# Splitting the attention exp by head, interleaving the causal mask, and moving four projection chunks in a fused attention and FFN kernel

## The chip, the cores and the metric

The kernel runs on the 8 cores of one Trainium2 chip. Each core takes one of the 8 batch elements, with the same program and the same weights, and no data passes between the cores. The metric is the device time in microseconds (us) of the slowest core.

## The reference

One layer on x of shape (8, 2048, 1024), with 16 heads of size 64 and an FFN of width 4096:

```python
def _L0_attn_ref(x, W_qkv, W_out):
    qkv = jnp.einsum('bsd,ndh->bnsh', x, W_qkv)
    q, k, v = jnp.split(qkv, 3, axis=-1)
    attn = jnp.einsum('bnqh,bnkh->bnqk', q, k) * scale      # scale = 1/8
    mask = -1e10 * (1.0 - jnp.tril(jnp.ones((S, S))))
    attn = jax.nn.softmax(attn + mask, axis=-1)
    out = jnp.einsum('bnqk,bnkh->bnqh', attn, v)
    out = out.reshape(B, -1, S)
    return jnp.einsum('bds,nhd->bsd', out, W_out)
...
x = x + _L0_attn_ref(_layernorm(x), L0_attn_W_qkv, L0_attn_W_out)
x = x + _L0_ffn_ref(_layernorm(x), w1, b1, w2, b2)          # relu FFN
```

The last einsum of the attention sums W_out over two of its indices, so it is a multiplication of each column of the output by one number (the kernel's WB_sb).

## The kernel before

The program has three stages. Up to about 165 us it normalizes x, transposes it to lnf_sb and computes V for all heads. From there to about 750 us it does attention, which is where the change lies. Then come the second layer norm and the FFN, in four groups of 512 tokens (L716 and L762 are its two matmuls).

Attention runs over 8 pairs of heads (npair 0 to 7). A pair has 40 steps, `steps = [(qb, j) ...]`: four query blocks qb of 512 queries, and for each the key blocks j of 128 keys up to the diagonal. Block 0 has steps 0 to 3, block 1 steps 4 to 11, block 2 steps 12 to 23, block 3 steps 24 to 39. The last four steps of a block are on the diagonal: they are 512, 384, 256 and 128 queries wide, and get a mask. For each step:

- `emit_se` gives TensorE the two score matmuls (L463), one a head. Head 0 lies in partitions 0 to 63 of kpair and qpair and head 1 in partitions 64 to 127, so each matmul uses half of the rows of the array. They write two neighbouring banks of PSUM. On a diagonal step two matmuls of 128 columns (L478, maskd times the identity, 128 rows) add the mask. Then one ScalarE activation (L491) takes exp of both heads and writes p_sb, a ring of three.
- `emit_pv` gives TensorE the two matmuls of P with V (L518), 128 rows each, one a head, into banks 4 and 5. vaug_h has 64 columns of ones beside V, so that these matmuls give the sum of the softmax too.

Scores have three regions of two banks (`REG_BASE`); a region is free when the exp of its step is done. All queues are in order. The order is written out by the loop at L591: a score step is emitted while fewer than three steps are ahead of PV, otherwise the next PV. So the queue of TensorE is SE0 SE1 SE2 PV0 SE3 PV1 and so on, and PV(k) comes right before SE(k+3). (SEk and PVk are names of this text for `emit_se(k)` and `emit_pv(k)`.)

`emit_epilogue`, called after the last PV of a block, copies banks 4 and 5 to oscr_sb with two VectorE copies (L534), then ScalarE does Ln (L544) and Exp (L550) to get the reciprocal of the sums, and VectorE multiplies (L558). The first PV of the next block waits for both copies. In the queue of ScalarE the Ln and Exp of a block that ends at step n stand before the exp of step n+3.

While pair p is in work, the Q and K projections of pair p+1 are done in eight chunks of eight matmuls (L375), two chunks at a time, in region 2. They stand at four places of the order, `ck_slots`; the two matmul groups of such a place are called CK0 to CK3 here. Each is followed by four VectorE casts (L391, L398), which must be done before region 2 is used again. Before the change CK0 to CK3 stand after PV8, PV16, PV24 and PV32.

At the start of a pair VectorE copies V (L418) and applies the previous pair's result to x ("permutes", L627 and L638, four times). The copies L534 of block 0 are behind these in VectorE's queue, and PV4 waits for them. Pair 7 has no next pair and so no chunks; pair 0 has no permutes before it.

Of the kernel before, what the change touches and what calls it, by code (L numbers as in the profile page):

```python
# [9 lines left out]
AF = mybir.ActivationFunctionType  # L10
ALU = mybir.AluOpType
AP = bass.AP
# [15 lines left out]
def build_program():  # L28
# [27 lines left out]
    def add(eng, emit, waits=(), inc=None, amt=1):  # L56
        w = [wt for wt in waits if wt[1] > 0]
        seq.append((eng, w, emit, inc, amt))
        if inc is not None:
            C[inc] += amt  # L60
            return C[inc]
        return None

    with ExitStack() as ctx:
# [4 lines left out]
        identb = sb("identb_sb", [128, 128], BF16)  # L69
        maskd = sb("maskd_sb", [128, 128], BF16)  # L70
# [8 lines left out]
        cst_sb = sb("cst_sb", [128, 3], F32)  # L79
# [4 lines left out]
        qpair = asb("qpair", [128, 2, S], BF16)  # L84
        kpair = asb("kpair", [128, 2, S], BF16)
        p_sb = asb("p_sb", [128, 3, 1024], BF16)
# [5 lines left out]
        arena = ctx.enter_context(nc.psum_tensor([128, 8, 512], F32))  # L92
        AR = 8 * 512
# [5 lines left out]
        for xq in range(4):  # L99
# [4 lines left out]
                waits=([(f"dq{xq - 1}", 16)] if xq > 0 else []),  # L104
                inc=f"dq{xq}", amt=16)
            dx_xq.append((f"dq{xq}", cnt))
        add("gpsimd", lambda e: e.dma_start(identb[:, :], identf_d.ap()),
            inc="dwb", amt=16)
        add("gpsimd", lambda e: e.dma_start(b2r_sb[:, :], b2_d.ap()),
            inc="dwb", amt=16)  # L110
        dx_consts = add("gpsimd", lambda e: e.dma_start(maskd[:, :],
                                                        maskd_d.ap()),
                        inc="dx", amt=16)
        for bcc in range(NWW):
# [3 lines left out]
                inc="dbc", amt=16)  # L118
# [52 lines left out]
        for kc2 in range(DC // 2):  # L171
# [5 lines left out]
            for r in range(2):  # L177
                kc = kc2 * 2 + r
                for h in range(2):
# [5 lines left out]
                                    start=(kc_ == 0), stop=(kc_ == DC - 1),  # L185
                                    skip_group_check=True))(sp + r, h, kc),
                                waits=[dw, ("vv", vv_ones)],
                                inc="mm" if h == 1 else None)
# [4 lines left out]
            waits=[("mm", wb_mm)], inc="vv")  # L193
# [144 lines left out]
        s_reg_free = [vv_lnf1, vv_vaug_done, ("ex", 0)]  # L338
        REG_BASE = [1024, 3072, 0]
        o_bank_free = [vv_vaug_done, vv_vaug_done]  # L340
        vv_attn_done = 0
        ex_attn_done = 0
# [66 lines left out]
        for npair in range(NH // 2):  # L409
            heads = (2 * npair, 2 * npair + 1)  # L410
            par = npair % 2
# [3 lines left out]
            vv_vh = 0  # L415
            for hix, n in enumerate(heads):
                vdrain()
                vv_vh = add("vector", (lambda n_, hx: lambda e: e.tensor_copy(  # L418
                    AP(vaug_h, hx * TC * 128, [[2 * TC * 128, 128],
                                               [128, TC], [1, 64]]),  # L420
                    AP(v_all, 64 * n_, [[TC * 1024, 128],
                                        [1024, TC], [1, 64]])))(n, hix),
                    waits=[vv_vaug_done, ("vv", vv_vones),
                           vaug_free[hix]],
                    inc="vv")
            if npair + 1 < NH // 2:
                next_chunks = make_qk_chunks(
                    npair + 1,
                    load_pair_slots((2 * npair + 2, 2 * npair + 3)))
            else:  # L430
                next_chunks = []
# [6 lines left out]
            ex_exp = {}  # L438
# [3 lines left out]
            def emit_se(si):  # L442
                nonlocal ex_attn_done
                qb, j = steps[si]
                qlo = max(128 * j, 512 * qb)
                qhi = 512 * (qb + 1)
                w = qhi - qlo
                off = qlo - 512 * qb
                reg = reg_of[si]
                base = REG_BASE[reg]  # L450
                reg_prev = s_reg_free[reg]
                ppar_guard = ([("mm", mm_pv[si - 3])] if si >= 3 else
                              ([("mm", p_guard[si % 3])]
                               if p_guard[si % 3] else []))
                mm_sc = None
                for hix in range(2):
                    w0 = [reg_prev] if hix == 0 else []
                    if si == 0 and hix == 0:
                        w0.append(("vv", vv_qk_done))
                    mm_sc = add("tensor",  # L460
                                (lambda j_, q_, w_, b_, hx, off_, p_:
                                 lambda e:
                                 e.matmul(  # L463
                                     AP(arena, b_ + hx * 512 + off_,
                                        [[AR, 128], [1, w_]]),
                                     kpair[hx * 64:(hx + 1) * 64, p_,
                                           j_ * 128:(j_ + 1) * 128],
                                     qpair[hx * 64:(hx + 1) * 64, p_,
                                           q_:q_ + w_],
                                     start=True, stop=True,  # L470
                                     skip_group_check=True))(
                                     j, qlo, w, base, hix, off, par),
                                waits=w0, inc="mm" if hix == 1 else None)
                if qlo == 128 * j:
                    for hix in range(2):
                        mm_sc = add("tensor",
                                    (lambda b_, hx, off_: lambda e:
                                     e.matmul(  # L478
                                         AP(arena, b_ + hx * 512 + off_,
                                            [[AR, 128], [1, 128]]),  # L480
                                         maskd[:, :], identb[:, :],
                                         start=False, stop=True,
                                         skip_group_check=True))(
                                         base, hix, off),
                                    waits=([("dx", dx_consts)]
                                           if hix == 0 else []),
                                    inc="mm" if hix == 1 else None)
                ew = [("mm", mm_sc)] + ppar_guard
                last_ex = add("scalar",
                              (lambda si_, w_, b_, off_: lambda e:  # L490
                               e.activation(  # L491
                                   AP(p_sb, (si_ % 3) * 1024,
                                      [[3 * 1024, 128], [512, 2], [1, w_]]),
                                   AP(arena, b_ + off_,
                                      [[AR, 128], [512, 2], [1, w_]]),
                                   AF.Exp, scale=cst_sb[:, 1:2]))(
                                   si, w, base, off),
                              waits=ew, inc="ex")
                s_reg_free[reg] = ("ex", last_ex)
                ex_exp[si] = last_ex  # L500
                ex_attn_done = last_ex

            def emit_pv(si):
                qb, j = steps[si]
                qlo = max(128 * j, 512 * qb)
                w = 512 * (qb + 1) - qlo
                off = qlo - 512 * qb
                jstop = 4 * qb + 3
                last = None
                for hix in range(2):  # L510
                    w0 = [("ex", ex_exp[si])] if hix == 0 else []
                    if j == 0 and hix == 0:
                        w0.append(o_bank_free[0])
                        w0.append(o_bank_free[1])
                        w0.append(("vv", vv_vh))
                    last = add("tensor",
                               (lambda j_, w_, hx, st_, si_, off_: lambda e:
                                e.matmul(  # L518
                                    AP(arena, (4 + hx) * 512 + off_,
                                       [[AR, 128], [1, w_]]),  # L520
                                    vaug_h[:, hx, j_ * 128:(j_ + 1) * 128],
                                    AP(p_sb, (si_ % 3) * 1024 + hx * 512,
                                       [[3 * 1024, 128], [1, w_]]),
                                    start=(j_ == 0), stop=st_,
                                    skip_group_check=True))(
                                    j, w, hix, j == jstop, si, off),
                               waits=w0, inc="mm" if hix == 1 else None)
                mm_pv[si] = last
                return last
# [40 lines left out]

            s_reg_free[2] = ("vv", vv_qk_pair[npair])
            rot = []
            ck_slots = {11, 20, 29, 38} if next_chunks else set()
            si_ctr = 0
            kk = 0
            rc = 0
# [14 lines left out]
            while npv < len(steps):  # L591
# [10 lines left out]
                else:  # L602
                    emit_pv(npv)
                    qb, j = steps[npv]
# [280 lines left out]
```

How the kernel before makes its waits and increments, by code:

```python
                def body(eng_obj):  # L834
                    last_wait = {}
                    for (e, waits, emit, inc, amt) in seq:
                        if e != eng_name:
                            continue
                        for wt in waits:
                            s_, v = wt[0], wt[1]
                            force = len(wt) > 2 and wt[2]
                            if v > 0 and (force or last_wait.get(s_, -1) < v):
                                eng_obj.wait_ge(sems[s_], v)
                                last_wait[s_] = max(last_wait.get(s_, -1), v)
                        if emit is None:
                            continue
                        inst = emit(eng_obj)
                        if inc is not None:
                            inst.then_inc(sems[inc], amt)
```

## Time and profile before

| | |
|---|---|
| median of 13 runs | 1323.79 us (1320.99 to 1426.11) |
| the profiled execution | 1321.26 us; its slowest core's span is 1319.7 us |
| spans of the 8 cores | 1308.7 to 1319.7 us |
| granted TensorE clock, mean of a core | 0.858 to 0.876 |
| TensorE matmul busy | 990.5 us, 75% |
| VectorE busy | 473.2 us, 36% |
| ScalarE busy | 414.9 us, 31% |
| exp of the scores (L491) | 320 activations, 294.3 us |

The span is from the first to the last instruction of a core; the other 1.6 us of the profiled execution lie around it. A row of the chain gives where a piece starts and how long it stays the thing that the end waits for. A row of the timeline gives start and length of a run of like instructions, and how long the engine idled before. A granted clock of 1.00 is 2.4 GHz, 0.50 is 1.2 GHz; TensorE is at one or the other.

### The profile page before, as it was taken

Reading aid. Unit: us, or ns where it says so; the run is one execution under the profiler, and the core shown is the slowest. Engines: PE = TensorE matmul, PEld = TensorE weight load, DVE = VectorE, ACT = ScalarE, POOL = GpSimd, SP = SyncE. Lnnn points to the kernel's source line nnn. Section 1 sums busy time; section 2 is a strip of 40 time slices with the busy share of each in tenths; the row PEclk is TensorE's granted clock in tenths of the full one; section 3 lists DMA queues with packets and bytes.
Section 4 is the critical chain, followed back from the end, with each engine's and each line's share of the span. In section 5 each row is a group of like instructions: output and inputs, shape, how many; then the busy total and the mean of one; then the engine's idle time right before and its main releaser. Section 6 shows DMA issues by size and latency. Waiting matters only on the chain.

```text
span 1319.7 us, 12768 instructions; the slowest of 8 cores (1308.7 to 1319.7 us)
## 1 busy us (share of the span) xinstructions
PE 990.5 (75%) x4656; PEld 392.7 (30%) x4656; DVE 473.2 (36%) x638; ACT 414.9 (31%) x443; POOL 80.1 (6%) x107
## 2 busy tenths in 40 slices
PE   1289788585858768595857277697899779987997
PEld 0134322131212222131212033243344334433443
DVE  0542323635363543635452632221342124212401
ACT  0134167475747657465658310001000100010000
POOL 2100200000000000000000000111001100110010
PEclk9589979797868879686878678798899889998999
DMA  8920701000000002000020059989538953895476
GB/s 190 183 11 1 72 9 16 1 9 8 9 8 1 1 0 32 1 1 0 1 32 1 1 111 209 179 140 171 161 114 129 161 167 118 125 159 164 127 116 140
DMA packets 102653, 101.59 MB, mean 77 GB/s; under 512 B 40128, under 2 KB 81088, under 8 KB 102592
## 3 DMA queue, kind: packets, MB, share of 16 engines
q0 software_dynamic: 60288, 50.41, 28.4%
q10 hardware_dynamic: 33280, 33.56, 8.2%
q1 hardware_dynamic: 9024, 16.80, 4.2%
q8 instruction: 40, 0.66, 0.2%
q14 instruction: 21, 0.17, 0.1%
HBM read 134.37 MB, written 16.78 MB: 115 GB/s over the span
## 4 chain that ended last, share of the span: by engine, by line
PE 64%; DVE 14%; DMA 13%; ACT 4%; issue 3%; DVEq 2%; POOL 0%; ACTq 0%; POOLq 0%
PE arena L762 17%; PE arena L716 14%; PE arena L518 11%; PE arena L375 9%; PE arena L463 6%; DMA wstage<-w1b 5%; DVE tmp_sb L627 5%; PE arena L297 5%; DVE oscr_sb L534 3%; DMA wstage<-w 3%; DVE x_sb L638 3%; DMA wstage<-wqkv 2%; DMA wstage<-wout 2%; PE arena L478 2%; DVEq L54 1%
## 5 line engine op out<-in xcount | busy, mean ns | idle before, releaser
L491 ACT ACTIVATE p_sb<-arena,cst_sb 128x1024 bf16<-128x1024 f32 (+1 forms) x320 | 294.3, 983 | 112.6 <-PE arena L463 71.9
L518 PE MATMUL arena<-p_sb,vaug_h 128*128 128x512 bf16 (+3 forms) x640 | 194.7, 392 | 150.2 <-DVE oscr_sb L534 96.1
L716 PE MATMUL arena<-lnf_sb,wstage 128*128 128x512 bf16 x1024 | 238.9, 397 | 57.9 <-DMA wstage<-w1b 36.2
L762 PE MATMUL arena<-w2stage,h_sb 128*128 128x512 bf16 x1024 | 221.7, 379 | 4.0 <-DVE h_sb L730 4.0
L730 DVE TENSOR_SCALAR h_sb<-arena,b1c_sb 128x512 bf16<-128x512 f32 x128 | 96.1, 751 | 210.5 <-PE arena L716 210.5
L716 PEld LDWEIGHTS arena<-lnf_sb,wstage 128*128 128x128 bf16 x1024 | 102.4, 101 | 193.5 <-issue 85.9
L762 PEld LDWEIGHTS arena<-w2stage,h_sb 128*128 128x128 bf16 x1024 | 99.9, 98 | 125.8 <-issue 5.9
L375 PE MATMUL arena<-lnf_sb,wstage 128*128 128x512 bf16 x512 | 130.1, 413 | 5.5 <-DMA wstage<-wqkv 5.5
L463 PE MATMUL arena<-qpair,kpair 64*128 64x512 bf16 (+3 forms) x640 | 126.3, 391 | 5.3 <-DVE kpair L398 5.3
L518 PEld LDWEIGHTS arena<-p_sb,vaug_h 128*128 128x128 bf16 x640 | 43.9, 101 | 211.5 <-issue 211.0
L391 DVE CAST qpair<-arena 64x512 bf16<-64x512 f32 x64 | 43.7, 683 | 171.5 <-PE arena L375 171.4
L799 DVE TENSOR_TENSOR y_sb<-arena,x_sb 128x512 f32<-128x512 f32 x32 | 19.5, 680 | 190.5 <-PE arena L776 190.5
L257 ACT ACTIVATE lnf_sb<-arena 128x1024 bf16<-128x1024 f32 x32 | 31.7, 1020 | 168.3 <-PE arena L249 168.3
L213 ACT ACTIVATE rsd_sb<-bag_sb,cst_sb 128x4 f32<-128x4 f32 x8 | 2.4, 296 | 253.4 <-DVE bag_sb L209 253.4
L534 DVE COPY oscr_sb<-arena 128x512 f32<-128x512 f32 x64 | 44.3, 692 | 98.3 <-PE arena L518 93.4
L375 PEld LDWEIGHTS arena<-lnf_sb,wstage 128*128 128x128 bf16 x512 | 53.8, 106 | 80.0 <-issue 31.5
L463 PEld LDWEIGHTS arena<-qpair,kpair 64*128 64x128 bf16 x640 | 31.5, 94 | 138.9 <-issue 134.7
L743 POOL DMA_DIRECT2D w2stage<-w x64 | 45.2, 708 | 423.1 <-PE arena L762 414.8
L558 DVE TENSOR_TENSOR onorm_sb<-oscr_sb,rec_sb 64x512 bf16<-64x512 f32 x64 | 41.1, 680 | 78.9 <-ACT rec_sb L550 78.9
L249 PE MATMUL arena<-identb_sb,lntm_sb 128*128 128x128 bf16 x256 | 24.4, 260 | 59.5 <-DVE lntm_sb L233 52.8
L297 PE MATMUL arena<-wstage,lnf_sb 128*128 128x512 bf16 x256 | 63.8, 406 | 3.4 <-DMA wstage<-wqkv 3.4
L544 ACT ACTIVATE rec_sb<-oscr_sb 64x1024 f32<-64x1024 f32 x32 | 33.7, 1054 | 94.6 <-DVE oscr_sb L534 94.6
(37 smaller groups left out, 442.7 us busy)
## 6 DMA issues: line engine op xcount, KB each, us to landing
w2stage<-w POOLq DMA_DIRECT2D x64, 512.0 KB, 6.4
wstage<-w1b ACTq DMA_DIRECT2D x24, 1024.0 KB, 7.1
x_sb<-x SPq DMA_DIRECT2D x4, 2048.0 KB, 14.5
wstage<-w POOLq DMA_DIRECT2D x8, 1024.0 KB, 11.9
w1b<-wstage ACTq DMA_DIRECT2D x8, 1024.0 KB, 8.4
y<-y_sb SPq DMA_DIRECT2D x16, 512.0 KB, 9.6
wstage<-wqkv POOLq DMA_DIRECT2D x24, 256.0 KB, 11.3
wstage<-wout POOLq DMA_DIRECT2D x4, 512.0 KB, 18.4
```

The lines of the kernel that those rows point to most:

```text
L297: (lambda s_, h_, dc_, c_, b_: lambda e: e.matmul(bankap(b_ + h_, 512), lnf_sb[:, dc_, c_ * 128:(c_ + 1) * 128], wstage[:, s_, h_ * 512:(h ...
L375: e.matmul(bankap(qb_, 512), wstage[:, s_, dc_ * 128: (dc_ + 1) * 128], lnf_sb[:, dc_, g_ * 512:(g_ + 1) * 512], start=(dc_ == 0), stop=(d ...
L391: e.tensor_copy(qpair[hx * 64:(hx + 1) * 64, pr, g_ * 512:(g_ + 1) * 512], bankap(qb_, 512, 0, 64)))(g, qb2, hix),
L463: e.matmul(AP(arena, b_ + hx * 512 + off_, [[AR, 128], [1, w_]]), kpair[hx * 64:(hx + 1) * 64, p_, j_ * 128:(j_ + 1) * 128], qpair[hx * 64 ...
L491: e.activation(AP(p_sb, (si_ % 3) * 1024, [[3 * 1024, 128], [512, 2], [1, w_]]), AP(arena, b_ + off_, [[AR, 128], [512, 2], [1, w_]]), AF. ...
L518: e.matmul(AP(arena, (4 + hx) * 512 + off_, [[AR, 128], [1, w_]]), vaug_h[:, hx, j_ * 128:(j_ + 1) * 128], AP(p_sb, (si_ % 3) * 1024 + hx ...
L534: vv_oc = add("vector", (lambda hx: lambda e: e.tensor_copy(AP(oscr_sb, hx * 512, [[1024, 128], [1, 512]]), AP(arena, (4 + hx) * 512, [[AR ...
L627: (lambda nn, h2_, hx: lambda e: e.tensor_mul(tmp_sb[h2_ * 64:(h2_ + 1) * 64, :, :], AP(onorm_sb, hx * S + h2_, [[2 * S, 64], [2, TC], [32 ...
L716: (lambda s_, dc_, fb_, wp_: lambda e: e.matmul(bankap(fb_, TF), AP(wstage, s_ * 1024 + dc_ * 512 + wp_ * 128, [[8 * 1024, 128], [1, 128]] ...
L730: vv_r = add("vector", (lambda ww_, fb_: lambda e: e.tensor_scalar(h1_sb[:, ww_, :], bankap(fb_, TF), b1c_sb[:, ww_:ww_ + 1], 0.0, op0=ALU ...
L743: (lambda sp_, ww_: lambda e: e.dma_start(AP(w2stage, sp_ * 1024, [[8 * 1024, 128], [1024, 2], [1, 1024]]), AP(w2_d, ww_ * 128 * D, [[D, 1 ...
L762: (lambda s_, ww_, c2_, dh_, t_: lambda e: e.matmul(bankap(t_, 512), h1_sb[:, ww_, 128 * c2_:128 * (c2_ + 1)], w2stage[:, s_, 512 * dh_:51 ...
```

## The change

Three edits, all in the attention of a pair:

1. `emit_se`: the exp of a step is two activations, one a head, each waiting for its own head's matmuls. Each score matmul raises the semaphore. On diagonal steps the order on TensorE is head 0 scores, head 0 mask, head 1 scores, head 1 mask (before: both scores, both masks). The region is free after the second exp.
2. `emit_pv`: the PV of each head waits for its own head's exp, and at a block's first step for the copy of its own bank.
3. `ck_slots` are 8, 17, 26, 35 in place of 11, 20, 29, 38. CK0 to CK3 now stand after PV5, PV13, PV21 and PV29.

```diff
-                mm_sc = None
+                mm_hx = [None, None]
                 for hix in range(2):
                     w0 = [reg_prev] if hix == 0 else []
                     if si == 0 and hix == 0:
                         w0.append(("vv", vv_qk_done))
-                    mm_sc = add("tensor",
...
-                                waits=w0, inc="mm" if hix == 1 else None)
-                if qlo == 128 * j:
-                    for hix in range(2):
-                        mm_sc = add("tensor",
...
-                                    waits=([("dx", dx_consts)]
-                                           if hix == 0 else []),
-                                    inc="mm" if hix == 1 else None)
-                ew = [("mm", mm_sc)] + ppar_guard
-                last_ex = add("scalar",
-                              (lambda si_, w_, b_, off_: lambda e:
-                               e.activation(
-                                   AP(p_sb, (si_ % 3) * 1024,
-                                      [[3 * 1024, 128], [512, 2], [1, w_]]),
-                                   AP(arena, b_ + off_,
-                                      [[AR, 128], [512, 2], [1, w_]]),
-                                   AF.Exp, scale=cst_sb[:, 1:2]))(
-                                   si, w, base, off),
-                              waits=ew, inc="ex")
-                s_reg_free[reg] = ("ex", last_ex)
-                ex_exp[si] = last_ex
-                ex_attn_done = last_ex
+                    mm_hx[hix] = add("tensor",
...
+                                     waits=w0, inc="mm")
+                    if qlo == 128 * j:
+                        mm_hx[hix] = add("tensor",
...
+                                         waits=([("dx", dx_consts)]
+                                                if hix == 0 else []),
+                                         inc="mm")
+                exs = [None, None]
+                for hix in range(2):
+                    exs[hix] = add("scalar",
+                                   (lambda si_, w_, b_, off_, hx: lambda e:
+                                    e.activation(
+                                        AP(p_sb,
+                                           (si_ % 3) * 1024 + hx * 512,
+                                           [[3 * 1024, 128], [1, w_]]),
+                                        AP(arena, b_ + hx * 512 + off_,
+                                           [[AR, 128], [1, w_]]),
+                                        AF.Exp, scale=cst_sb[:, 1:2]))(
+                                        si, w, base, off, hix),
+                                   waits=[("mm", mm_hx[hix])] + ppar_guard,
+                                   inc="ex")
+                s_reg_free[reg] = ("ex", exs[1])
+                ex_exp[si] = exs
+                ex_attn_done = exs[1]
...
-                    w0 = [("ex", ex_exp[si])] if hix == 0 else []
-                    if j == 0 and hix == 0:
-                        w0.append(o_bank_free[0])
-                        w0.append(o_bank_free[1])
-                        w0.append(("vv", vv_vh))
+                    w0 = [("ex", ex_exp[si][hix])]
+                    if j == 0:
+                        w0.append(o_bank_free[hix])
+                        if hix == 0:
+                            w0.append(("vv", vv_vh))
...
-            ck_slots = {11, 20, 29, 38} if next_chunks else set()
+            ck_slots = {8, 17, 26, 35} if next_chunks else set()
```

## Rows read from the trace of the kernel before

**Rows 1.** Spans and clocks of the cores: the slowest one.

```profile
core 1: 1319.7 us, clock 0.858
```

**Rows 2.** The chain in order of time, 529 to 610 us (pair 5).

```profile
544.69 1.01 PE arena L518 x2
...
556.37 0.39 PE arena L463 x2
556.77 0.23 PE arena L518 x2
...
558.78 0.59 PE arena L518 x2
...
560.90 1.10 ACT p_sb L491
...
565.24 4.43 PE arena L375 x16
...
570.53 0.32 PE arena L463 x2
...
571.77 0.22 PE arena L478 x2
...
573.99 0.32 PE arena L463 x2
...
574.96 0.23 PE arena L518 x2
...
577.67 5.03 PE arena L375 x16
...
590.00 3.45 PE arena L375 x16
...
598.62 0.69 DVE oscr_sb L534
```

**Rows 3.** Groups of instructions by shape: exp (busy us, mean ns of one).

```profile
L491 ACT ACTIVATE p_sb<-arena,cst_sb 128x1024 bf16<-128x1024 f32 x224 | 234.4, 1111 | 72.0 <-PE arena L463 71.9
...
L491 ACT ACTIVATE p_sb<-arena,cst_sb 128x512 bf16<-128x512 f32 x32 | 21.9, 685 | 0.7 <-PE arena L478 0.2
```

**Rows 4.** Timeline, 575 to 606 us: exps, and TensorE's matmuls of one step.

```profile
583.13 8.15 ACT L491 ACTIVATE p_sb<-arena,cst_sb 128x1024 bf16<-128x1024 f32 x8 [2.94 <-PE arena L463]
...
583.50 0.39 PE L463 MATMUL arena<-qpair,kpair 64*128 64x512 bf16 x2
...
583.82 0.60 PE L518 MATMUL arena<-p_sb,vaug_h 128*128 128x512 bf16 x2
...
584.36 0.39 PE L463 MATMUL arena<-qpair,kpair 64*128 64x512 bf16 x2
```

**Rows 5.** Timeline of TensorE in pair 7, 722 to 726 us.

```profile
722.13 0.59 PE L518 MATMUL arena<-p_sb,vaug_h 128*128 128x512 bf16 x2 [1.59 <-ACT p_sb L491]
...
723.13 0.59 PE L518 MATMUL arena<-p_sb,vaug_h 128*128 128x512 bf16 x2
```

**Rows 6.** Stretches: length, busy of PE, PEld, DVE, ACT, POOL, then the clock.

```profile
544.69:549.98 5.29, 5.29 (x17) 1.17 (x18) 1.29 (x2) 5.21 (x6) 0.00 (x0) 0.50 0.00 0
...
563.60:567.04 3.44, 3.44 (x10) 1.15 (x10) 0.00 (x0) 2.40 (x3) 0.00 (x0) 0.51 0.02 5
...
720.00:734.10 14.10, 11.85 (x62) 3.38 (x60) 1.29 (x2) 13.71 (x15) 0.00 (x0) 1.00 0.01 2
```

**Rows 7.** The whole chain in order of time: L627 after pairs 0 and 6.

```profile
232.72 1.87 DVE tmp_sb L627
...
680.05 1.87 DVE tmp_sb L627
```

**Rows 8.** The chain in pair 0, 150 to 232 us: PV4 and the last copies.

```profile
174.06 1.01 PE arena L518 x2
...
226.37 0.69 DVE oscr_sb L534
```

More of the change, by code:

```diff
@@ L459, in emit_se @@
                         w0.append(("vv", vv_qk_done))
-                    mm_sc = add("tensor",
[L461 to L472, printed above, removed]
-                                waits=w0, inc="mm" if hix == 1 else None)
@@ L474, in emit_se @@
-                if qlo == 128 * j:
-                    for hix in range(2):
-                        mm_sc = add("tensor",
[L477 to L484, printed above, removed]
-                                    waits=([("dx", dx_consts)]
-                                           if hix == 0 else []),
-                                    inc="mm" if hix == 1 else None)
@@ L499, in emit_se @@
-                s_reg_free[reg] = ("ex", last_ex)
-                ex_exp[si] = last_ex
-                ex_attn_done = last_ex
+                    mm_hx[hix] = add("tensor",
+                                     (lambda j_, q_, w_, b_, hx, off_, p_:
+                                      lambda e:
+                                      e.matmul(
+                                          AP(arena, b_ + hx * 512 + off_,
+                                             [[AR, 128], [1, w_]]),
+                                          kpair[hx * 64:(hx + 1) * 64, p_,
+                                                j_ * 128:(j_ + 1) * 128],
+                                          qpair[hx * 64:(hx + 1) * 64, p_,
+                                                q_:q_ + w_],
+                                          start=True, stop=True,
+                                          skip_group_check=True))(
+                                          j, qlo, w, base, hix, off, par),
+                                     waits=w0, inc="mm")
@@ new lines, in emit_se @@
+                    if qlo == 128 * j:
+                        mm_hx[hix] = add("tensor",
+                                         (lambda b_, hx, off_: lambda e:
+                                          e.matmul(
+                                              AP(arena,
+                                                 b_ + hx * 512 + off_,
+                                                 [[AR, 128], [1, 128]]),
+                                              maskd[:, :], identb[:, :],
+                                              start=False, stop=True,
+                                              skip_group_check=True))(
+                                              base, hix, off),
+                                         waits=([("dx", dx_consts)]
+                                                if hix == 0 else []),
+                                         inc="mm")
@@ new lines, in emit_se @@
+                exs = [None, None]
[6 more added lines that the diff above has]
+                                           [[3 * 1024, 128], [1, w_]]),
+                                        AP(arena, b_ + hx * 512 + off_,
+                                           [[AR, 128], [1, w_]]),
+                                        AF.Exp, scale=cst_sb[:, 1:2]))(
+                                        si, w, base, off, hix),
+                                   waits=[("mm", mm_hx[hix])] + ppar_guard,
+                                   inc="ex")
```

## The prediction

> **What bounds the kernel now.** I read the spans of the cores first: the slowest is core 1, at 1319.7 us [rows 1], and its trace stands for the time. The profiled execution took 1321.3 us; the median of the runs lies 2.5 us above it, and the sum below is made against the 1321.3. Only the attention changes. Its chain in order of time [rows 2] shows what a pair is made of: PV4 restarts TensorE at 544.69, when VectorE has worked off the permutes, and the pair's last copies start at 598.62, 53.9 us later. The other 21 us of the 75 are Ln, Exp and VectorE's permutes, which the edits don't touch. So only the 53.9 us can change.
>
> Inside them two engines take turns. One wide step costs TensorE 0.86 us (583.50 to 584.36 [rows 4]). Its exp takes 1.11 us, but eight in a row fill 8.15 us: one each (8.15 - 1.11)/7 = 1.01 us, so neighbours overlap by 0.10. ScalarE is the slower one, but it catches up while a CK occupies TensorE (it idled 2.94 us there [rows 4]). In pair 7, which has no CK, PVs come every 1.00 us [rows 5]: exp is the bound. Behind each block TensorE waits for the copies (PV11 ends at 557.00, PV12 starts at 558.78), and then for the exp of step n+3, queued behind Ln and Exp: it starts at 560.90, 3.9 us after PV11's end [rows 2]. Third, the clock. TensorE restarts at 0.50 after the permutes and stays there 5.3 us; it falls to 0.50 again at 563.60, for 3.44 us [rows 6], and a second time in block 3. Both falls follow idle spots of 1.5 us. CK1 and CK2 then take 4.43 and 5.03 us against 3.45 for CK3 [rows 2]; the two falls cost pair 5 some 3.2 us (half of 6.8 slow us, less what stalls hid).
>
> **The split exp.** 320 activations become 640. The row for 512 elements says 685 ns, that for 1024 says 1111 [rows 3]. With the same overlap of 0.10, two halves come every 2 x 0.58 = 1.16 us against 1.01: +0.15 us a step, 49 us on ScalarE in all. On the path it counts only where ScalarE is the bound. In return the first PV can start some 0.5 us before the second half is done, and the first half starts 0.1 to 0.4 us sooner; that shortens an idle spot once a stretch, not once a step.
>
> **The order on diagonal steps.** Two score matmuls of 512 columns cover 0.39 us where two PVs cover 0.60, and from the first score to the first PV only 0.32 us pass [rows 4], where 1024 columns at 2.4 GHz need 0.427. So the two heads' scores, in different halves of the rows, run side by side, and a wide step is 0.213 (scores) + 0.427 (PVs) + 2 x 0.11 for the changes between half-row and full-row matmuls. The masks use all rows and stand behind both scores, 0.22 us for two [rows 2]. In the new order a full-row mask stands between the scores: they can't run together (+0.213, 0.160, 0.107 and 0.053 us for the four widths, 0.53 in all), and there are four changes of form where there were two (+0.21 a step, 0.86 in all). Four diagonal steps took 3.46 us (570.53 to 573.99 [rows 2]) and take 4.85: +1.39. No row shows a mask alone between two scores, so the second part lies between 0 and 0.86; I take 0.86, since 0.11 shows at both changes of every wide step. Block 0's four lie under the permutes and cost nothing; three fours a pair can count.
>
> The Trainium skill, page "TensorEngine Tiling (Array Packing)", section Key Properties, says that changing the tiling mode, not just the tile, drains the engine. By that rule the changes are drains and the upper end holds; without it the lower end would. The 0.11 of this trace agrees with it.
>
> **The split copy wait.** The first PV of a block starts after the first copy, 0.78 us sooner (0.69 [rows 2] and its queue). Half a PV (0.21 us, 0.5 at the slow clock) is done when the second copy lands.
>
> **The chunks.** CK1 moves from behind PV16 to behind PV13, so it covers the wait for exp 14. CK2 moves from behind PV24, where it covered the wait for exp 26, to behind PV21, where it doesn't. One covered wait is gained, one lost. In VectorE's queue CK2's casts now stand before block 2's copies: the last two come at the end of CK2 + 0.2 and last 1.4, and PV23 ends 1.1 after CK2, so the copies, and PV24 and Ln behind them, start 0.3 us late. Casts must also be done before the third step behind a CK. Behind CK0 that step waited 0.3 us, since narrow steps followed (556.37 [rows 2], after VectorE); now wide ones follow and the wait is gone. The weight loads on POOL wait for the last chunk of each head, are issued a pair ahead, and come free sooner: nothing waits for them.
>
> **The sum for pair 5.** A, from PV4 to the end of PV11 at 557.00: 12.3 us, -0.5 (half of PV4 done), -0.3 (casts), +1.4 (diagonal) = 12.9. B, to the end of PV23 at 575.19, 18.2 us before, counted from PV11's end: first PV at 1.0, PV13 ends 2.9, CK1 to 6.4, PV14 to PV17 at 0.86 each to 9.8 (the exps, from 6.7 at 1.16, are just in time), four diagonal steps 4.85 to 14.7 (TensorE the bound), CK2 to 18.15, two scores and two narrow PVs to 19.25. C, to the last copies, 23.4 us before: 0.3 late, exp 26 starts 3.9 later, then exp sets the pace: PV29 ends 9.3 after PV23 (28.6), CK3 to 32.05, ten more exps at 1.16, less for the narrow ones, the last held a little by TensorE's masks, to 40.7. B and C took 41.5, of which 3.2 was the clock; now 40.7 at the full clock. One place has idle enough for a fall, the start of block 3 (0.7 + 0.5 + 1.5 us within 5); a slow 3.4 us costs 1.1 there (a step at 0.50 is 1.73 us against 1.16). So 41.8, with A 54.7 against 53.8: +0.9.
>
> The other pairs: L627 at 232.72 and 680.05 gives (680.05 - 232.72)/6 = 74.55 us a pair [rows 7], where pair 5 has 75.1; the others have in part fewer slow stretches. The new pair is 75.1 + 0.9 = 76.0: +1.45 x 6 = +8.7. Pair 0 needs 52.3 us from PV4 to the copies [rows 8], the new one 54.7: +2.4. Pair 7 has no CK: +1.2 in A (diagonal, half of it at the slow clock), +1.5 in B (seven wide exps at +0.15, masks behind), +2.0 in C (eleven wide exps and masks): +4.7. Sum 15.8. 1321.3 + 15.8 = 1337.1, and with the 2.5 to the median 1339.
>
> **The rivals.**
> - Changes of form cost nothing, but the scores no longer run together: A loses 0.86, B 0.85, and 2 in pair 7, -14: 1325, no difference. For it: TensorE partly waits for exp in these stretches anyway. Against: the 0.11 at every change in rows 4.
> - Not slower: the diagonal order is free altogether, the masks hiding in the waits for exp, and the earlier starts remain: A -1.4, B -1.0, C -0.1, with pair 7 -19: 1320. It decides when four diagonal steps cost under 0.4 us more (under 0.1 for a gain of 0.3%). Against: in A TensorE never waits, so nothing can hide.
> - The clock gets worse: exps at 1.16 us leave TensorE 26% idle, and with the spots at the blocks each pair gets one or two more slow stretches at 1.1 to 1.7 us: 1347 to 1363. For it: 1.5 us of idle was enough twice. Against: in pair 7 the same spots at a pace 14% idle left the clock at 1.00 [rows 6].
> - The clock gets better: no fall behind PV4, -1.1 x 7, and a restart that leaves 0.50 sooner than after 5.3 us [rows 6], up to -1.7 x 7: 1331 to 1320.
>
> **How the numbers follow.** Forecast 0.50, free changes of form 0.13, free diagonal 0.08, worse clock 0.15, better clock 0.11, others 0.03. 0.3%, 4 us, is about what a measurement of this kernel can tell from no change. Faster (under 1319.8): half of free diagonal, a third of better clock, others: 0.11. Same: 0.16. Slower (over 1327.8): 0.73. Range 1321 to 1356: from the free diagonal to one more slow stretch a pair at its upper price with some over. The forecast's own range is 1330 to 1345.
>
> **What the profile would show.** L491: 640, ScalarE busy +65 us or more (2 x 0.685 against 1.11). In pair 7, PVs every 1.16 us. Four diagonal steps at 4.85 us where TensorE is the bound, the two scores of one no longer together. CK1 at 3.45 us. L627 every 76.0 us. I am wrong if two halves come faster than 1.16 us, if masks between the scores cost nothing, or if the clock stands at 1.00 much longer or shorter than I count.

## The result

The changed kernel takes 1338.8 us (median of 11 runs, 1337.7 to 1342.2); the kernel before, with the runs made beside it, 1325.0. The ratio is 1.0104, 95% interval 1.0085 to 1.0123: slower by 1%. The forecast was 1339 against 1323.8, a ratio of 1.0115. The profiled execution took 1342.1 us; its slowest core is 0. In some executions of every kernel here the cores of one die show a lower granted clock and the time is some per cent longer; the medians are of all executions, the ratios leave those out.

### The profile page after: what moved, and what is told of

It is laid out like the page before. It is cut to its first block, busy times and chain, and to the rows that moved or that the text cites. A ratio compares the mean times of both kernels' runs of the same rounds, so it can differ in the third digit from the quotient of the medians.

```text
span 1340.6 us, 13665 instructions; the slowest of 8 cores (1325.7 to 1340.6 us)
## 1 busy us (share of the span) xinstructions
PE 1043.7 (78%) x4656; PEld 415.4 (31%) x4656; DVE 472.6 (35%) x638; ACT 461.7 (34%) x763; POOL 80.2 (6%) x107
## 4 chain that ended last, share of the span: by engine, by line
PE 68%; DVE 12%; DMA 11%; ACT 3%; issue 3%; DVEq 2%; POOL 0%; ACTq 0%; POOLq 0%
PE arena L765 17%; PE arena L719 16%; PE arena L521 11%; PE arena L375 9%; PE arena L463 7%; DVE tmp_sb L630 4%; PE arena L297 4%; DMA wstage<-w 3%; DVE x_sb L641 3%; DMA wstage<-wqkv 3%; DVE oscr_sb L537 3%; PE arena L477 2%; DMA wstage<-w1b 2%; DMA wstage<-wout 2%; DVEq L54 1%
## 5 line engine op out<-in xcount | busy, mean ns | idle before, releaser
L492 ACT ACTIVATE p_sb<-arena,cst_sb 128x512 bf16<-128x512 f32 (+3 forms) x640 | 341.2, 637 | 90.9 <-PE arena L463 58.5
L521 PE MATMUL arena<-p_sb,vaug_h 128*128 128x512 bf16 (+3 forms) x640 | 207.8, 402 | 116.3 <-DVE oscr_sb L537 78.7
L719 PE MATMUL arena<-lnf_sb,wstage 128*128 128x512 bf16 x1024 | 239.7, 399 | 54.8 <-DMA wstage<-w1b 32.5
L463 PE MATMUL arena<-qpair,kpair 64*128 64x512 bf16 (+3 forms) x640 | 169.4, 401 | 5.4 <-DVE kpair L398 4.9
L375 PE MATMUL arena<-lnf_sb,wstage 128*128 128x512 bf16 x512 | 123.4, 397 | 9.4 <-DMA wstage<-wqkv 9.4
L521 PEld LDWEIGHTS arena<-p_sb,vaug_h 128*128 128x128 bf16 x640 | 48.7, 101 | 193.5 <-issue 191.7
L537 DVE COPY oscr_sb<-arena 128x512 f32<-128x512 f32 x64 | 44.3, 692 | 131.3 <-PE arena L521 124.9
L463 PEld LDWEIGHTS arena<-qpair,kpair 64*128 64x128 bf16 x640 | 43.2, 94 | 141.3 <-issue 129.8
L802 DVE TENSOR_TENSOR y_sb<-arena,x_sb 128x512 f32<-128x512 f32 x32 | 19.5, 680 | 190.4 <-PE arena L779 190.4
```

The lines of the kernel that those rows point to most:

```text
L375: e.matmul(bankap(qb_, 512), wstage[:, s_, dc_ * 128: (dc_ + 1) * 128], lnf_sb[:, dc_, g_ * 512:(g_ + 1) * 512], start=(dc_ == 0), stop=(d ...
L463: e.matmul(AP(arena, b_ + hx * 512 + off_, [[AR, 128], [1, w_]]), kpair[hx * 64:(hx + 1) * 64, p_, j_ * 128:(j_ + 1) * 128], qpair[hx * 64 ...
L492: e.activation(AP(p_sb, (si_ % 3) * 1024 + hx * 512, [[3 * 1024, 128], [1, w_]]), AP(arena, b_ + hx * 512 + off_, [[AR, 128], [1, w_]]), A ...
L521: e.matmul(AP(arena, (4 + hx) * 512 + off_, [[AR, 128], [1, w_]]), vaug_h[:, hx, j_ * 128:(j_ + 1) * 128], AP(p_sb, (si_ % 3) * 1024 + hx ...
L537: vv_oc = add("vector", (lambda hx: lambda e: e.tensor_copy(AP(oscr_sb, hx * 512, [[1024, 128], [1, 512]]), AP(arena, (4 + hx) * 512, [[AR ...
L719: (lambda s_, dc_, fb_, wp_: lambda e: e.matmul(bankap(fb_, TF), AP(wstage, s_ * 1024 + dc_ * 512 + wp_ * 128, [[8 * 1024, 128], [1, 128]] ...
```

## The profile after

The head of the page and the rows of its engines (busy us, share of the span, instructions):

```profile
span 1340.6 us, 13665 instructions; the slowest of 8 cores (1325.7 to 1340.6 us)
PE 1043.7 (78%) x4656; PEld 415.4 (31%) x4656; DVE 472.6 (35%) x638; ACT 461.7 (34%) x763; POOL 80.2 (6%) x107
```

TensorE has the same 4656 matmuls and is busy 53 us longer; ScalarE has 320 activations more and 47 us more. Taken over all cores, attention (first projection matmul to the start of the last L627, now L630) took 602.5 us on average before and takes 619.1: +16.6. What lies before it and behind it differs by 1.5 and 0.4 us. So the slowdown is in attention, as forecast.

The chain in order of time, pair 6: CK1, one diagonal step at the full clock, CK2, the first of the two copies of block 2, CK3, and the first of the two copies of block 3 (L521 is the PV, L477 the mask and L537 the copy of this kernel):

```profile
650.07 3.45 PE arena L375 x16
...
657.10 0.32 PE arena L463
657.42 0.16 PE arena L477
657.58 0.32 PE arena L463
657.90 0.16 PE arena L477
658.07 0.43 PE arena L521 x2
...
661.93 3.47 PE arena L375 x16
...
667.11 0.69 DVE oscr_sb L537
...
676.70 3.45 PE arena L375 x16
...
689.19 0.69 DVE oscr_sb L537
```

Each score now holds the path for 0.32 us, where the two together held it for 0.32 before [rows 4]: 0.213 of columns and 0.107 of a change of form (from full-row to half-row matmuls or back). A mask holds it 0.16, 0.053 and again 0.107. The four steps of block 2 go from 657.10 to 661.93, 4.83 us; before 3.46 [rows 2]. All three chunk groups shown run at the full clock, where CK1 and CK2 took 4.43 and 5.03 us before. The timeline of the same step shows the scores as single runs of one, apart by 0.48 us, where before both started together:

```profile
657.04 0.39 PE L463 MATMUL arena<-qpair,kpair 64*128 64x512 bf16 x1
657.36 0.23 PE L477 MATMUL arena<-identb_sb,maskd_sb 128*128 128x128 bf16 x1
657.52 0.39 PE L463 MATMUL arena<-qpair,kpair 64*128 64x512 bf16 x1
```

The exps, by shape, and a run of eight of them with no wait between, in pair 7's timeline:

```profile
L492 ACT ACTIVATE p_sb<-arena,cst_sb 128x512 bf16<-128x512 f32 x448 | 266.1, 692 | 75.8 <-PE arena L463 58.5 <-PE arena L477 17.3
```

```profile
741.66 4.68 ACT L492 ACTIVATE p_sb<-arena,cst_sb 128x512 bf16<-128x512 f32 x8
```

(4.68 - 0.69)/7 = 0.57 us each, 1.14 a step against 1.00 in that pair before [rows 5].

The clock, by stretches (length, busy of the engines, then the clock). First two stretches of pair 6, then four of pair 7, each 4 us, counted from 710.3, where the PV starts that waited for the second copy (the half PV before it starts at 709.5):

```profile
640.00:666.00 26.00, 24.82 (x123) 9.06 (x121) 9.38 (x15) 19.11 (x35) 0.00 (x0) 1.00 0.00 1
...
668.80:675.70 6.90, 6.46 (x17) 1.06 (x16) 1.29 (x2) 6.83 (x11) 0.00 (x0) 0.51 0.00 0
```

```profile
710.29:714.29 4.00, 3.98 (x11) 0.87 (x11) 1.29 (x2) 3.93 (x6) 0.00 (x0) 0.50 0.01 2
718.29:722.29 4.00, 4.00 (x18) 1.04 (x16) 0.00 (x0) 2.30 (x6) 0.00 (x0) 0.50 0.00 0
722.29:726.29 4.00, 3.33 (x11) 0.64 (x10) 1.38 (x2) 3.30 (x6) 0.00 (x0) 0.50 0.00 0
726.29:730.29 4.00, 3.69 (x11) 0.67 (x10) 1.28 (x2) 4.00 (x9) 0.00 (x0) 0.50 0.00 0
```

In a pair with chunks the clock falls once behind the restart, at the start of block 3, where it was expected; it stays down for 6.8 us in 29 of the 48 pairs (pairs 1 to 6 of the eight cores) and for 3.4 us in 19, where 3.4 was counted. In pair 7 it stays at 0.50 for 20 us on every core. For the first 12 of them TensorE is never idle; then comes the wait for block 1's copies. And the first L630 behind pairs 0 and 6, in the whole chain:

```profile
241.45 1.87 DVE tmp_sb L630
...
695.54 1.87 DVE tmp_sb L630
```

(695.54 - 241.45)/6 = 75.7 us a pair, against 74.55 [rows 7].

The three stretches, from copies to copies (A from the start of the PV that waits for block 0's second copy, B and C from the start of block 1's and 2's copies), on the profiled slowest core. The forecast counted to the ends of PV11 and PV23; here it is put on the same marks, the copies starting 0.16 us behind PV11, and 0.16 + 0.3 behind PV23:

| | before, pair 5 | after, pair 6 | forecast | before, pair 7 | after, pair 7 |
|---|---|---|---|---|---|
| A | 12.5 | 12.5 | 13.1 | 8.7 | 12.2 |
| B | 18.2 | 19.9 | 19.5 | 13.6 | 15.4 |
| C | 23.3 | 22.1 | 22.1 | 17.1 | 19.1 |
| sum | 53.9 | 54.5 | 54.7 | 39.5 | 46.8 |

What a fall of the clock costs can be read in the kernel before by itself, since not every pair has one. B and C of pair 3 of core 2, where it falls in both, and of pair 4, where it doesn't:

```profile
408.14:426.30 18.16, 14.96 (x73) 4.92 (x72) 5.42 (x8) 12.99 (x14) 0.00 (x0) 0.91 0.00 1
426.30:449.56 23.26, 21.09 (x100) 7.28 (x100) 8.18 (x12) 16.56 (x18) 0.00 (x0) 0.93 0.00 0
483.11:499.82 16.71, 13.43 (x73) 4.58 (x72) 5.42 (x8) 12.99 (x14) 0.00 (x0) 1.00 0.00 1
499.82:522.01 22.19, 19.53 (x100) 6.86 (x100) 8.19 (x13) 16.66 (x18) 0.87 (x1) 1.00 0.16 22
```

The fall in B costs 1.5 us and the one in C 1.1, together 2.6, where the prediction put 3.2. Of the 48 pairs with chunks the clock falls in B in 45 and in C in 36; B is 16.7 and C 22.2 in all the others.

## The experiments

Each is timed against the kernel before in the same session; "ratio" is to that kernel. Phases are as in the table, for a pair late in the kernel (5 or 6) where nothing else is said; counts are over pairs 1 to 6 of the eight cores, 48 in all.

**e1_old_order.** The changed kernel with the old order on diagonal steps.

```diff
-                    if qlo == 128 * j:
-                        mm_hx[hix] = add("tensor",
+                if qlo == 128 * j:
+                    for hix in range(2):
+                        mm_hx[hix] = add("tensor",
```

> The changed kernel with one part undone: on diagonal steps both score matmuls come first and then both masks, as before; exps, waits and chunks stay as changed. Theory (the order keeps the two heads' scores from running together and adds two changes between half-row and full-row matmuls): four diagonal steps fall from 4.83 us back to 3.46 where TensorE is the bound, about 2.5 us a pair and 2 or more in pair 7, 19 us in all: 1320 to 1324 us, a ratio to the kernel before of 0.997 to 1.000. In pair 7 TensorE leaves the clock of 0.50 within some 5 us of its restart, where the changed kernel needs 20. Rival (the doubled exps are the cost, the masks' order hides behind them): 1333 to 1339 us, ratio 1.007 or more.

1319.2 us, ratio 0.9955 (0.9938 to 0.9972), at the lower edge of what was expected. Between it and the changed kernel lie 19.6 us, and the order is all that differs. Without it, the remaining edits make the kernel 0.4% faster. Its pair 7, the first 8 us behind the restart:

```profile
693.15:697.15 4.00, 3.43 (x10) 0.78 (x11) 1.28 (x2) 3.94 (x6) 0.00 (x0) 0.50 0.01 2
697.15:701.15 4.00, 4.00 (x25) 1.45 (x24) 0.00 (x0) 4.00 (x10) 0.00 (x0) 0.83 0.01 4
```

The clock rises in the second 4 us, as before the change (within 4.0 to 6.0 us of the restart on all eight cores); A of pair 7 is 8.5 us, not 12.2.

**e2_order_only.** The kernel before with the new diagonal order alone.

```diff
+                    if qlo == 128 * j:
+                        mm_hx[hix] = add("tensor",
...
-                ew = [("mm", mm_sc)] + ppar_guard
+                ew = [("mm", mm_hx[1])] + ppar_guard
```

> The kernel before with one part of the change: scores and mask of head 0, then of head 1, on diagonal steps; one exp a step, which waits for the last mask; chunks and waits as before. Theory: TensorE is the bound in all three diagonal fours that can count, since a chunk group stands just before two of them, so +1.4 us for each, 4.2 us a pair, and some 5 in pair 7 with its clock: +20 to +34 us, ratio 1.015 to 1.026. Rival (the order hides): within 5 us of before.

1358.8 us, ratio 1.0258 (1.0240 to 1.0275), within what was expected. A grows from 12.5 to 15.7 us, more than the 1.4 of the four steps. The chain of its core 2 shows why: masks and scores behind the restart run at the slow clock, and so does half of CK0 behind them.

```profile
572.07 1.01 PE arena L518 x2
...
576.96 0.43 PE arena L463
577.39 0.22 PE arena L477
577.62 0.43 PE arena L463
578.05 0.22 PE arena L477
578.27 0.85 PE arena L518 x2
...
581.07 2.53 PE arena L375 x8
```

Two PVs at 0.85 are the slow clock (0.43 at the full one), and 8 matmuls in 2.53 us are more than the 1.73 of the full clock. The clock leaves 0.50 only 9 to 11 us behind the restart in every pair with chunks (2.8 to 6.1 us before) and after 17 to 18 us in pair 7 (3.4 to 5.9 before). B and C, 18.1 and 23.6, look as if the order were nearly free there, against 18.2 and 23.3. It isn't: without a fall they were 16.7 and 22.2, and 1.4 each is the price of four steps. What hides it is that the falls that cost 1.5 and 1.1 are gone: in this kernel the clock doesn't fall in C at all, and in B, in 32 of 48 pairs, only at its start, where B is as long as without a fall. So the time came as expected in part because A lost more and B and C less. In the change itself CK0 stands ahead of these steps, so the loss is smaller there: 1.5% (e1 to the change) against 2.6% alone.

**e3_exp_only.** The kernel before with two exps a step, each waited for by its own PV.

```diff
-                    w0 = [("ex", ex_exp[si])] if hix == 0 else []
+                    w0 = [("ex", ex_exp[si][hix])]
```

and the two activations of the change.

> The kernel before with one part of the change: two exps a step, one a head, each waited for by its own PV; diagonal order, copy wait and chunks as before. Theory: a wide step costs ScalarE 1.14 us against 1.00, but only the last four or so steps between two chunk groups are bound by it, and the head start of the first half gives some back: 1 to 2 us a pair, 3 in pair 7 (22 wide steps at 0.14): +8 to +17 us, ratio 1.006 to 1.013. Rival (halves let PV start sooner and hide the rest): within 4 us of before.

1330.1 us, ratio 1.0042 (1.0026 to 1.0057): a loss, but below the range expected. Pair 7 loses its 3 us (42.5 against 39.5); the pairs with chunks lose next to nothing (53.3 to 54.8 against 53.9, by the core). Their C does lose 0.9 to 1.0 us, 23.1 against 22.2 without a fall of the clock and 24.3 against 23.3 with one; but the clock falls in C in 15 of 48 pairs, where it did in 36.

**e4_slots_only.** The kernel before with the chunk groups at the new places.

```diff
-            ck_slots = {11, 20, 29, 38} if next_chunks else set()
+            ck_slots = {8, 17, 26, 35} if next_chunks else set()
```

> The kernel before with one part of the change: chunk groups behind PV5, PV13, PV21 and PV29. Theory: the wait for the exp behind Ln and Exp is covered at the start of block 2 and bare at the start of block 3, one for one, and the casts of the third group hold up the copies of block 2 by 0.3 us a pair; the clock can fall once less: -7 to +5 us, ratio 0.995 to 1.004. Rival (the places are the cost of the change): +10 us or more.

1305.4 us, ratio 0.9850 (0.9833 to 0.9868). Both expectations missed: the places are the large gain of the change, 20 us. A pair takes 50.5 us from restart to last copies, against 53.9: 11.9, 18.7 and 19.9. Before, B and C are 16.7 + 22.2 = 38.9 us where the clock doesn't fall and 41.5 where it falls twice; here they are 38.6. So most of the gain, 2.6 of 3.4 us, is the cost of the clock; A, with its wait for the casts gone, gives 0.6. The chain of core 4, its CK1 and CK3, the stretch at the start of block 3 where the clock falls, and C of a pair without a fall (pair 2) and of this one (pair 5):

```profile
551.17 3.45 PE arena L375 x16
...
575.37 3.45 PE arena L375 x16
```

```profile
565.50:570.70 5.20, 3.43 (x14) 0.71 (x12) 2.44 (x4) 4.38 (x5) 0.00 (x0) 0.75 0.00 0
...
351.86:371.77 19.91, 16.31 (x84) 5.30 (x85) 5.42 (x8) 15.88 (x17) 0.87 (x1) 1.00 0.15 14
566.80:586.71 19.91, 17.61 (x84) 5.35 (x85) 5.42 (x9) 15.88 (x17) 0.00 (x0) 0.91 0.00 1
```

The clock still falls once in half of the pairs, but over waits for copies and exp, where it costs nothing: C is 19.9 with such a fall of 3.4 us (24 pairs) and without (22 pairs). Before, it fell over the start of CK1 and CK2 (4.43 and 5.03 us against 3.45).

**e5_bank_only.** The kernel before; at a block's first step each PV waits for its own bank's copy.

```diff
-                    if j == 0 and hix == 0:
-                        w0.append(o_bank_free[0])
-                        w0.append(o_bank_free[1])
-                        w0.append(("vv", vv_vh))
+                    if j == 0:
+                        w0.append(o_bank_free[hix])
+                        if hix == 0:
+                            w0.append(("vv", vv_vh))
```

> The kernel before with one part of the change: at a block's first step the PV of each head waits only for the copy of its own bank. Theory: half a PV is done when the second copy lands, 0.2 us at the full clock and 0.5 at the slow one, three times a pair: about -0.9 us a pair, -6 us, ratio 0.995; the shorter idle spots may save a fall of the clock, then down to 0.985. Rival (the PV of head 1 needs the second copy anyway, nothing is gained): within 3 us of before.

1331.8 us, ratio 1.0040 (1.0026 to 1.0053): slower by 0.4%, where a gain of 0.5% was expected. The rows are of core 0. A pair still takes 54.0 us, but A is 14.0, B 17.8 and C 22.2, where they were 12.5, 18.2 and 23.3, and pair 7 takes 42.1 against 39.5. Its pair 5, from the restart on (TensorE at 0.50 for 5.3 us there before [rows 6]):

```profile
545.30:549.30 4.00, 3.59 (x11) 0.61 (x10) 1.29 (x2) 3.93 (x4) 0.00 (x0) 0.50 0.00 0
549.30:553.00 3.70, 3.70 (x15) 1.28 (x15) 0.00 (x0) 2.72 (x4) 0.00 (x0) 0.50 0.00 0
```

The clock stays at 0.50 for at least 7.7 us, and in every pair of every core for 8 to 9.5. The half PV was won and a longer slow start lost; in C the clock no longer falls. Why it rises later these runs don't show.

**e8_slots_bank.** The kernel before with the edits of e4 and e5.

> The two parts of the change that run alone did not make slower: chunk groups behind PV5, PV13, PV21, PV29, and each PV waiting for its own bank's copy; one exp a step and the old diagonal order. Places alone gave 0.985. If the gains add, 0.978 to 0.982 (1296 to 1301 us); if the places have already removed the falls of the clock that the split wait could save, 0.982 to 0.985.

1320.2 us (1308 to 1340; 1308 to 1312 in the executions that the ratio counts), ratio 0.9881 (0.9864 to 0.9897). That is 0.3% worse than e4 alone, whose interval this one just touches, and outside both ranges expected. In its profiled run the pairs take 50.5 to 51.9 us, 50.5 in e4, and pair 7 42.8 against 40.9. The clock now falls in C in every pair, in 22 of 48 for 6.8 us, and C is 20.8 to 22.3 against 19.9. From here to e1, which adds the split exp, is +0.7%.

**e7_after_one_exp.** The changed kernel with one exp a step.

```diff
-                exs = [None, None]
-                for hix in range(2):
-                    exs[hix] = add("scalar",
+                ew = [("mm", mm_hx[1])] + ppar_guard
+                last_ex = add("scalar",
```

> The changed kernel with one part undone: one exp a step again, waiting for the last mask; the split diagonal order, the split copy wait and the moved chunks stay. Theory (the order is the main cost, the exps a small one): 0 to 8 us below the changed kernel, ratio to the kernel before 1.004 to 1.010. In pair 7 the clock stays at 0.50 for some 20 us after the restart, as in the changed kernel, since the order is the cause. Rival (doubled exps are the cost): ratio 0.998 or less, and the clock recovers early.

1343.3 us (1338 to 1346 in the executions that the ratio counts), ratio 1.0116 (1.0095 to 1.0137): above the range expected, and not told apart from the changed kernel's 1.0104. Beside the new order, the doubled exps cost nothing that can be measured, TensorE being the bound. Its pair 7 on core 3, stretches as above:

```profile
709.56:713.56 4.00, 3.98 (x11) 0.88 (x11) 1.28 (x2) 3.93 (x4) 0.00 (x0) 0.50 0.00 0
717.56:721.56 4.00, 4.00 (x18) 1.03 (x16) 0.00 (x0) 2.21 (x4) 0.00 (x0) 0.50 0.00 0
725.56:729.56 4.00, 3.27 (x10) 0.48 (x8) 1.28 (x2) 4.00 (x5) 0.00 (x0) 0.50 0.00 0
```

The long slow stretch is here too, with one exp (23 us on four of the cores, 13 on the others), and is absent in e1, with two. e2, the order alone, has it too (17 to 18 us), and no kernel with the old order has more than 9.2 us in pair 7 (e5, the split copy wait): it comes with the order.

**e10_ck1_only** and **e11_ck0_only.** One group moved: `{11, 17, 29, 38}` and `{8, 20, 29, 38}`.

> The kernel before with one chunk group moved: the second from behind PV16 to behind PV13; the others stay behind PV8, PV24 and PV32. Theory (a chunk group behind the copies' wait covers the wait for the exp behind Ln and Exp, and as dense work keeps TensorE's clock up): block 2 loses its bare wait of 1.5 us and both falls of the clock in a pair go, 3 to 5 us a pair, 21 to 35 us: ratio 0.974 to 0.985. Rival (the gain of the moved places comes from the first group or the cast wait behind it): ratio 0.995 or more.

> The kernel before with one chunk group moved: the first from behind PV8 to behind PV5; the others stay. Theory: only the cast wait of 0.3 us goes, the falls of the clock stay: -2 to -5 us, ratio 0.996 to 0.999. Rival (this group is what gains): ratio 0.988 or less.

e10: 1315.9 us, ratio 0.9902 (0.9865 to 0.9939), runs from 1306 to 1346: between the range expected and the rival. In its profiled run most pairs take 50.5 us, while on cores 6 and 7 the first two take 54 to 57, at 0.50 for about half of that time; core 6 sets the time, and why they are slow is open. Half of the mechanism is as expected: the bare wait of block 2 is gone, and so is the fall in C (in 4 of 48 pairs it is left). The other fall is not gone. In 38 of 48 pairs the clock falls at the start of block 2, and the moved CK1 runs in part at 0.50, on core 0 so:

```profile
552.98 4.27 PE arena L375 x16
```

B is 16.5 with this fall and 14.9 without, those slow cores apart (18.2 before). e11: 1317.9 us, ratio 0.9944 (0.9919 to 0.9969): more than the cast wait, outside the range expected. Its pairs vary from 51 to 53.5 us, with B at 16.7 in some and 18.2 in others: shifting the first group also shifts where the clock falls.

**e6_cover_both** and **e9_cover_no_bank.** A new order of the chunks, with and without the split copy wait; the rest as before the change.

```diff
-            ck_slots = {11, 20, 29, 38} if next_chunks else set()
+            ck_slots = {8, 17, 29, 38} if next_chunks else set()
```

> A new version: one exp, old diagonal order, split copy wait, chunk groups behind PV5, PV13, PV24 and PV32, so that the wait for the exp behind Ln and Exp is covered at the start of block 2 and of block 3 too. Theory: the bare wait of 1.5 us at the start of block 3 goes (10 us over 7 pairs) and with it idle that lets the clock fall: 1286 to 1297 us, ratio 0.972 to 0.980. Rival (what made the moved places good is that a dense group follows each idle spot late enough): the clock falls on the third group again, 5 us a pair at most lost, ratio 0.985 to 0.995.

> The version with both waits covered, chunk groups behind PV5, PV13, PV24 and PV32, but with the old copy wait (both PVs of a block's first step wait for both copies). The split copy wait alone made the kernel slower (1.004) and took something from the moved places too. Theory (by starting TensorE early with half a PV it delays the clock's rise after the permutes): without it the time is 1282 to 1289 us, ratio 0.967 to 0.973. Rival (with both waits covered the split wait gains): 1290 to 1297 us.

e6: 1289.8 us, ratio 0.9733 (0.9718 to 0.9748), within the range expected and the fastest. e9: 1296.4 us, ratio 0.9786 (0.9763 to 0.9809): here the split wait gains 6.5 us, the rival's case. In e6 the clock falls in none of the 48 pairs; in e9 it falls in B in 17, which take 16.5 us there and not 14.9. Chain of e6, core 2, one pair: the copies of blocks 0 to 3 and CK0 to CK2.

```profile
590.84 0.69 DVE oscr_sb L534
...
594.55 4.30 PE arena L375 x16
...
603.67 0.69 DVE oscr_sb L534
...
606.52 3.45 PE arena L375 x16
...
618.39 0.69 DVE oscr_sb L534
...
640.56 0.69 DVE oscr_sb L534
```

CK0, behind the restart, still runs in part at the slow clock (4.30 us for 16 matmuls); CK1 has the full one (3.45). B is 14.7 us, C 22.2, and a pair 48 us, against 53.9.

## Why the prediction was right, step by step

- **The order on diagonal steps** was the cost, as forecast. Four steps took 4.83 us, forecast 4.85, with both parts as priced: no scores together, and 0.107 at each change of form. Its worth inside the change was put at 19 us (the rival of a free order: 1339 to 1320) and measured at 19.6 (e1, 1319.2). The total fits better than its parts: pair 7 alone gives 4.2 us of it (46.8 to 42.6), through the clock, where the rival counted some 1.5. Both rivals that made the order cheaper are out.
- **The split exp**: 1.14 us a step, forecast 1.16. That it costs only where ScalarE is the bound held too (e3 +0.4%, 3 of its 4.4 us in pair 7; e7). ScalarE's busy time was overrated, +47 us against +65 or more: the busy time counts the overlap of neighbours once.
- **The chunks**: the sum had them right, the reasoning about them alone did not. The sum took the 3.2 us of clock a pair out and put 1.1 back; the falls had cost 2.6, and the one that is left costs nothing in e4. The expectation for e4, written from the two covered and uncovered waits, left most of that out and missed 20 us. One wait is covered and one bared, so what these places change is the clock; in e6, which covers both waits, the waits count too.
- **The split copy wait** was the step that failed. It was booked at -0.5 us a pair; alone it made the kernel 0.4% slower, through the clock (e5), and with the chunks of e6 it gained 0.5%. Its sign hangs on where the clock rises and falls: alone it keeps the restart slow for 3 us more, with e6's chunks it goes with a B that has no fall.
- **The clock** was left as it was at the restarts, and it was not. In pairs with chunks it rises after 2.9 to 6.4 us, most often after less than 4, where 5.3 was counted: A is 12.5 instead of 13.1. The fall in block 3 lasts 6.8 us where 3.4 was counted, and C still came out right. Both rivals on the clock are in part true, and they cancel in part.
- **Pair 7** was forecast at +4.7 and lost 7.3. B and C came near what was worked out (+1.8 and +2.0 against 1.5 and 2.0), B with luck, since its first 8 us are at 0.50, which the sum didn't have; A lost 3.5 instead of 1.2, because of the 20 us at 0.50. Pair 0: 54.6 us, forecast 54.7. The others: 75.7 a pair, forecast 76.0. These misses of +2.6 and 6 x -0.3 nearly cancel: that the total is within 2 us of the forecast is luck in part.
- The four parts alone add up to +2.6 +0.4 -1.5 +0.4 = +1.9%, all together +1.0%. They are not independent: the moved CK0 takes away much of what the order costs behind the restart (slow for 9 to 11 us in e2, for 3 to 6 in the changed kernel).

## What to carry to other kernels

Two half-row matmuls that run side by side lose it as soon as a full-row matmul is put between them, even a small one; look at whether both start together in the timeline before reordering them. A dense group of matmuls is worth most where it covers a wait and where the clock doesn't fall on it: the same fall of 3.4 us cost 1.1 to 1.6 us over a chunk group (the kernel before, e10) and nothing over waits (e4). Look for both in the clock by stretches after every move. And time a change in parts: here one edit cost 20 to 33 us and hid that another gained 20.

## What the runs showed of the hardware that was not expected

In the changed kernel, TensorE being busy all the time doesn't bring the clock back. In the new order pair 7 has it at 0.50 for 20 us, with 3.3 to 4.0 us busy in every 4 and no idle spot in the first 12; in the old order, with 3.4 us busy in the first 4, it rises within 4 to 6 us of the restart (e1). The Trainium skill, page "TensorE: Matmul & The Clock Gate", section "Why this matters for your kernels", gives keeping TensorE continuously busy as the way to the full clock: those first 12 us of pair 7 of the changed kernel don't agree with it. Whether the half-row matmuls or the changes of form keep it down was not tried. Also not settled is why the clock rises later in e5.
